# A two-layer graph network on one core: one more wait ahead of each gather of layer two

## The reference

```
messages   = relu(concat(x[src], x[dst]) @ W_msg + b_msg)        # one row of 256 per edge
aggregated = segment_sum(messages, dst)                          # summed per destination node
h          = relu(concat(x, aggregated) @ W_upd + b_upd)
out        = layernorm(h) * gamma + beta, then layernorm(x + out)
```

## Time and profile before

| | us |
|---|---|
| median of 3 timed runs | 4386.48 |
| lowest and highest | 4386.21, 4386.79 |
| the profiled execution, its span | 4403.8 |
| first gather of layer two starts | 1946.0 |
| last gather of layer two starts | 4339.0 |
| TensorE busy | 3810.6 (87%) |
| VectorE busy | 3380.9 (77%) |
| ScalarE busy | 2779.1 (63%) |
| GpSimd busy | 2477.9 (56%) |

### The profile page before, as it was taken

One profiled execution on the slowest core, in us unless ns is written; L12 is line 12 of the kernel. 1 busy time (PEld: TensorE's weight loads), 2 busy tenths in 40 slices (PEclk: granted clock), 3 DMA queues, 4 the chain that ended last, 5 costly groups with the idle time before them and its releaser, 6 DMA issues.

```text
span 4403.8 us, 85804 instructions
## 1 busy us (share of the span) xinstructions
PE 3810.6 (87%) x26341; PEld 3176.6 (72%) x26341; DVE 3380.9 (77%) x7638; ACT 2779.1 (63%) x7247; POOL 2477.9 (56%) x2585
## 2 busy tenths in 40 slices
PE   4999999899999999956888888878888888888886
PEld 4999999788888888845666666666666666666665
DVE  7999999799999999955666666666666666666666
ACT  4888888777777777744555555555555555555554
POOL 2653655344455555536666666666666666666662
PEclk8999999999999999988899999999999989999998
DMA  5776544567777777743444444444444444444442
GB/s 133 243 231 226 190 189 188 197 191 206 209 209 209 209 209 208 206 141 110 127 142 129 136 127 140 132 130 136 131 132 136 135 131 131 128 129 139 131 131 72
DMA packets 344434, 707.82 MB, mean 161 GB/s; under 512 B 58153, under 2 KB 201334, under 8 KB 343954
## 3 DMA queue, kind: packets, MB, share of 16 engines
q0 software_dynamic: 114912, 359.18, 29.2%
q1 hardware_dynamic: 229074, 343.13, 23.1%
HBM read 507.96 MB, written 195.74 MB: 160 GB/s over the span
## 4 chain that ended last, share of the span: by engine, by line
PE 44%; DVE 29%; issue 11%; another core or an unknown queue 9%; ACT 2%; DVEq 2%; DMA 2%; SPq 1%; POOL 0%; ACTq 0%; POOLq 0%
PE ps L1327 11%; PE ps L1339 10%; DVE big L1903 7%; PE ps L1157 6%; DVE scr L1753 4%; PE ps L1305 4%; DVE arena L1913 3%; DVE arena L1756 3%; PE ps L1219 2%; PE ps L1164 2%; PE ps L1230 2%; PE ps L1188 2%; DVE scr L1756 1%; PE ps L1147 1%
## 5 line engine op out<-in xcount | busy, mean ns | idle before, releaser
L795 POOL DMA_INDIRECT arena<-d_p,tabs x1612 | 1543.0, 957 | 890.8 <-issue 457.3
L1913 DVE TENSOR_TENSOR arena<-arena,ps 128x512 f32<-128x512 f32 x806 | 527.0, 683 | 760.9 <-remote 503.8
L1327 PE MATMUL ps<-arena 128*128 128x256 f32 x3224 | 897.3, 419 | 240.1 <-DVE big L1903 174.2
L1111 ACT ACTIVATE arena<-arena 128x1024 f32<-128x1024 f32 x403 | 425.7, 1056 | 1004.8 <-DVE arena L1913 956.3
L1339 PE MATMUL ps<-big,scr 128*128 x3224 | 840.3, 401 | 219.6 <-DVE arena L1913 134.4
L1327 PEld LDWEIGHTS ps<-arena 128*128 128x128 f32 x3224 | 627.7, 205 | 424.2 <-ACT arena L1111 192.3
L1339 PEld LDWEIGHTS ps<-big,scr 128*128 128x128 f32 x3224 | 641.9, 202 | 356.9 <-issue 261.1
L1903 DVE SCALAR_TENSOR_TENSOR big<-big,tabs,ps 128x256 f32 x1612 | 767.8, 476 | 105.7 <-DVE big L1903 47.7
L781 POOL DMA_INDIRECT arena<-d_m,scr x392 | 531.2, 1355 | 564.0 <-DVE arena L1756 220.8
L1305 PE MATMUL ps<-arena,scr 128*128 128x256 f32 x2620 | 614.9, 384 | 10.5 <-DVE arena L1756 10.3
L1305 PEld LDWEIGHTS ps<-arena,scr 128*128 128x128 f32 x2620 | 483.7, 190 | 93.2 <-issue 32.9
(11 more groups left out here) (285 smaller groups left out, 5753.3 us busy)
## 6 DMA issues: line engine op xcount, KB each, us to landing
d_m<-arena SPq DMA_DIRECT2D x108, 603.0 KB
arena<-d_loc SPq DMA_DIRECT2D x135, 384.0 KB
d_m<-arena SPq DMA_DIRECT2D x108, 402.0 KB
arena<-d_p,tabs POOLq DMA_INDIRECT x1612
arena<-in_xT_dram SPq DMA_DIRECT2D x96, 256.0 KB
d_xp<-arena SPq DMA_DIRECT2D x49, 256.0 KB, 3.3
arena<-d_xp SPq DMA_DIRECT2D x49, 256.0 KB
d_x<-arena SPq DMA_DIRECT2D x49, 256.0 KB
```

Source lines behind the costliest of these rows:

```text
L795: e.indirect_dma_start(out=G1[j % 8][:, k, :], out_offset=None, in_=d_p, in_offset=bass.IndirectOffsetOnAxis(ap=tabS[:, j, k:k + 1], axis= ...
L1111: e.activation(G1[g % 8], G1[g % 8], ACT.Relu).then_inc(S("f_re"), 1)
L1327: m = e.matmul(turn(H, AB)[:, k * 256:k * 256 + 256], OH1[(j - 2) % 4][:, 2 * h + k, :], G1[(j - 2) % 8][:, 2 * h + k, :], start=True, sto ...
L1913: e.tensor_tensor(v, v, q2(turn(2 * j + h, QB)[:, :]), ALU.add).then_inc(S("f_m"), 1)
```

## The change

The first gather of group j also waits until VectorE has finished both halves of the message of group j - 3:

```diff
             def gath(j, g, i):
                 waitn(e, "f_ag", 2 * (j - 7))
+                waitn(e, "f_m", 2 * (j - 2))
                 for k in range(4):
                     e.indirect_dma_start(out=G1[j % 8][:, k, :], out_offset=None, in_=d_p,
```

## The result

The changed kernel took 4575.53 us (median of 4 runs, 4572.5 to 4578.26), the kernel before 4386.64 us beside it: ratio 1.0424, interval 1.0404 to 1.0444. The forecast was 4575. A second batch gave 4574.88 against 4381.1, ratio 1.0443 (1.0424 to 1.0462); one run of the kernel before in it, 5069.56 us at a granted clock of 0.701, is left out. The profiled execution has a span of 4576.7 us.

A forecast was written before the change was run, and what follows sets the result against it. GpSimd's gather issue plus its pauses, ended by late TensorE signals, was taken to bound layer two. Profiled 4403.8 + 205 (longer restarts, grown runs) - 14 (end) = 4595, less 17.3 for the median: 4577, stated 4575; range 4340 to 4740.

The forecast's parts named there:

- What bounds: Layer two: GpSimd's gathers set the length, 5.04 us a group without pause; 361 us of pauses are the loss.
- The loop: Layer two: GpSimd's long runs hold up TensorE's signals; it stops, signals arrive 1.8 to 2.4 us later, it restarts.
- Term 1: GpSimd's restart after a pause: 2.04 us from the message's start, 1.7 us more; +326 us at the same 192 pauses.
- Term 2: Longer pauses let more messages pass, so gather runs grow, at most 3 groups: +205 us, bounds +102 and +350.
- Term 3: Layer's two ends: only 3 groups instead of 6 left behind the last gather, -14 us; start already counted.
- Term 4: Gathers where no pause stands: the new wait is free, taken at nothing, upper bound +96 us.
- The sum: Profiled run: 4403.8 + 205 - 14 = 4595 us; timed median 17.3 us below, so 4577, stated as 4575.
- (a): Rival: holding GpSimd back lets TensorE's signals through, so long waits never form; faster, 4190 us, 25%.
- (b): Rival: nothing happens, slack absorbs the later gather start; 4386 us, less up to 14 at the end, 12%.

The follow-up runs named there:

- lead 2 on TensorE's signal: Kernel before, its gather wait drawn from the aggregation of the eighth group back to the fourth: 4372.01 us, ratio 0.9966, signals late.
- the first half alone: Kernel before, its aggregation wait replaced by one for the first half of the message of the third group back: 4454.49 us, ratio 1.0167, signals late.
- the message of the second group back: Kernel before plus a gather wait for the message of the second group back, one group tighter than the change: 4549.39 us, ratio 1.0386, signals late.
- its relatives: Variants of the kernel before with the message wait alone, first half added, or aggregation of fifth group back: ratios 0.9997, 0.9999, 0.9999, signals on time.

## Why the prediction was right

**What bounds.** Right in the condition in which it was made. GpSimd's total is the layer's length: the gathers' stretch grew by 182 us and the spans by 173. What was not seen, and could not be from one trace, is that the pauses are not a property of the kernel: with the signals on time the same code takes 348 us less, which is about the 361 us that the prediction set as all pauses.

**The loop.** Half shown. GpSimd's full issue is needed for the late signals (half of the gathers: 8.8 us of unknown waits where the kernel before beside it takes 4388 us), although run length and traffic were changed together there. The first long wait ends near the run's end (29.15 and 14.19 us at the start, with 36 and 20 gathers). Over the whole layer of the kernel before, 180 halves of messages started after a wait and over 3 us behind their query product, 129 of them inside a pause of GpSimd, though pauses are 18% of the time; the other 51 came while it ran, so the rule that signals come when GpSimd stops is not strict. Long runs are not enough either (on time, 1612 gathers without a pause). The second ingredient is open: the same chip was in one condition in one batch and in the other in another.

**Term 1, the restart.** 2.04 us from the message's start was forecast, 2.06 measured, with 0.78 against 0.76 for two waits. That the restart is the price is shown by lead 2 on TensorE's signal (4372 us with the changed kernel's lead, against 4575), and in size by the first half alone: the same kind of wait on VectorE, a restart 1.10 us shorter, 120 us less. How the 1.10 us divides in time between the second wait and the second half was not measured, since the two runs that take one of them each met signals on time; the restarts say 0.50 and 0.60 to 0.69.

**Term 2, the runs grow.** Right in direction: 225 pauses became 150, with 12 gathers as the common run, and the mean pause went from 1.90 to 3.83 us, 1.93 more where 1.7 was taken. The stretch rose by 182 where +205 was taken, 6.39 us a group instead of 6.45. The count of 192 pauses was too low, since waits whose end the profile cannot place are listed under "issue". And its reason for the upper end of a run, the limit of the lead, is refuted by the message of the second group back.

**Term 3, the ends.** -14 forecast, -14.4 measured.

**Term 4.** The wait is free where there is no pause, its extra instruction included: gathers that follow without one stand 0.306 us apart after and 0.305 before.

**The sum.** The profile's +191 became +172.9; that the median came out at 4575.5 for 4575 owes 16 us to luck, since the profile before was 17.3 us above its median and the profile after 1.2: the forecast of the profiled span, 4595, was 18 us too high, and the 17.3 us taken off it were 16 too many.

**Rivals.** (a), faster because the pauses let the signals through, did not come: the unknown waits grew to 818.9 us. The one case in which signals came through where the kernel before has them late had gathers taken away, not held back. (b), no change, is what its relatives do when the signals are on time, for the reason given against it: there are no pauses to lengthen. The Trainium skill's rule in "DMA: Bandwidth & Descriptors", Rules for kernel authors, holds in its own field: a gather 3 groups ahead is still early enough, and in the changed kernel only 0.5 us of waiting is for gathers. The time went where the rule does not look, into the issuing engine. The Trainium skill's "SBUF — State Buffer", Who interferes with whom, speaks of ports, and no run here shows a port conflict. Nor is TensorE's own work shown to wait; what comes late is its signal to others, and that does depend on how much GpSimd issues (503.8 against 8.8 us of unknown waits).

## What to carry to other kernels

When an engine only issues transfers and its total equals the length of the stage, look at how it is restarted: here a restart on the signal of the engine that frees the buffer cost less than one that goes by way of a third engine, and a restart with one wait 0.5 us less than one with two. If the lead is to be limited, do it by that same signal: the aggregation of the fifth group back gives a lead of 3 to 4 groups and 4368 us, 0.5% below the kernel before when signals are late and equal to it when they are not; that of the fourth group back gives 2 and 4372 us. And before a price is believed, time the kernel before in more than one batch: 4387 and 4035 us are the same code.

## What the runs showed of the hardware

- TensorE's signals can come late while GpSimd issues indirect DMAs: 180 halves of the kernel before started after a wait and over 3 us (5.6 us in the median, 34.8 at most) behind the recorded end of their query product, while ScalarE got VectorE's signal within 0.04 us. In other batches, with the same instructions, TensorE's counts were recorded within 0.02 us of the matmul's end. Why is open.
- A GpSimd gather starts 0.27 us after the recorded end of VectorE's message when it has one wait, 0.77 us when it has two (medians over 145 and 150 pauses). The second wait is an instruction of its own: 395 more instructions at 395 gathers with two waits.
- 128 rows of 1 KB by an indirect DMA have landed 2.8 us after the gather's start in the median, by the semaphore, with the signals on time.
